# Local attention layers: steps of two head pairs, block transposes on VectorE, value products on 32x64 tiles

## The reference, cut to what matters

```python
def local_attention(q, k, v):                 # per head, nw = 8 windows of w = 32 queries
    bk2, bv2 = look(bk), look(bv)             # own window and the one before: 64 keys
    sim = einsum('bhwie,bhwje->bhwij', bq, bk2) * 8
    sim = where(mask, -max, sim)
    attn = softmax(sim, -1)
    return einsum('bhwij,bhwje->bhwie', attn, bv2)
def attn_layer(x, Wqkv, qs, ksc, Wo):
    q, k, v = split(x @ Wqkv)                 # 128 -> 3 x 1024
    q, k = l2norm(q) * qs, l2norm(k) * ksc    # then rotary tables with a scale
    ...
    return local_attention(q, k, v) @ Wo
def ffn_layer(x, g, bln, W1, b1, W2, b2):
    xn = layernorm(x) * g + bln
    a, gate = split(xn @ W1 + b1)             # 2 x 341
    return a * gelu(gate) @ W2 + b2
for i in range(6):
    x = attn_layer(shift_tokens(x)) + x
    x = ffn_layer(shift_tokens(x)) + x
```

## Time and profile before

| | us |
|---|---|
| median of 3 runs | 3802.07 (3801.65 to 3807.49) |
| the profiled execution, span | 3799.8 |
| first raw rows of the stage | near 1905 |
| one unit in the steady part | 38.18 |

### The profile page before, as it was taken

How to read it: one execution, slowest core, us unless ns; L and a number is a source line. 1 busy time by engine, 2 the same in 40 slices (tenths; PEclk the granted TensorE clock), 3 DMA queues, 4 the chain that set the end, 5 groups by cost and what they waited for, 6 DMA issues and landing times.

```text
span 3799.8 us, 102343 instructions
## 1 busy us (share of the span) xinstructions
PE 3156.4 (83%) x41325; PEld 2042.2 (54%) x41325; DVE 2683.2 (71%) x7106; ACT 2234.7 (59%) x5603; POOL 1457.8 (38%) x1443
## 2 busy tenths in 40 slices
PE   7878876727767879877679999999999999999997
PEld 5544544612323546545446666666666666666665
DVE  6466656537896554579787878777777777777773
ACT  4234442426554332268757777777777777777775
POOL 0110011336572000000066665656665666565651
PEclk9989987968897989989899999999999999999997
DMA  1000002710000000000001011101110201111110
GB/s 54 1 5 1 2 12 54 228 65 0 0 1 5 2 1 1 14 17 1 30 21 32 22 32 51 32 22 42 41 32 22 61 22 29 54 29 24 28 26 22
DMA packets 50453, 108.05 MB, mean 28 GB/s; under 512 B 7376, under 2 KB 17488, under 8 KB 48192
## 3 DMA queue, kind: packets, MB, share of 16 engines
q1 hardware_dynamic: 47456, 96.33, 9.3%
q0 software_dynamic: 2528, 5.18, 0.7%
HBM read 52.27 MB, written 5.18 MB: 15 GB/s over the span
## 4 chain that ended last, share of the span: by engine, by line
PE 45%; DVE 23%; ACT 13%; issue 6%; POOL 3%; DMA 1%; POOLq 0%; SPq 0%; DVEq 0%; ACTq 0%
PE psum L3240 5%; PE psum L3297 5%; PE psum L403 5%; PE psum L3280 4%; PE psum L1218 4%; PE psum L3190 4%; PE psum L408 3%; PE psum L2071 3%; DVE scratch L3452 2%; DVE xnT L3606 2%; PE psum L1272 2%; DVE xnT L3489 2%; ACT L3356 1%; PE psum L3265 1%; DVE scratch L3454 1%
## 5 line engine op out<-in xcount | busy, mean ns | idle before, releaser
L3646 POOL TENSOR_TENSOR scratch<-scratch 128x512 f32<-128x512 f32 x384 | 488.4, 1272 | 409.1 <-DVE scratch L3455 409.1
L408 PEld LDWEIGHTS psum<-table,scratch 128*128 128x128 f32 (+1 forms) x2284 | 283.1, 145 | 294.2 <-issue 234.1
L3297 PE MATMUL psum<-weights,scratch 128*128 128x512 f32 x768 | 413.6, 621 | 15.0 <-ACT y L3392 14.5
L408 PE MATMUL psum<-table,scratch 128*128 128x128 f32 (+1 forms) x2284 | 370.1, 283 | 44.5 <-DVE scratch L2772 11.8
L3659 POOL TENSOR_TENSOR scratch<-scratch,xnT 128x512 f32<-128x512 f32 x384 | 402.2, 1047 | 0.0
L3452 DVE TENSOR_TENSOR scratch<-psum,xnT 128x512 f32<-128x512 f32 x384 | 264.3, 688 | 146.0 <-PE psum L3297 139.4
L3426 ACT COPY scratch<-psum 128x512 f32<-128x512 f32 x384 | 225.8, 588 | 155.7 <-PE psum L408 149.8
L3392 ACT ACTIVATE y<-psum 128x512 f32<-128x512 f32 x384 | 230.9, 601 | 104.9 <-DVE scratch L3455 91.9
L3606 DVE TENSOR_REDUCE xnT<-y 128x8 f32<-128x512 f32 x384 | 253.9, 661 | 1.4
L1218 PE MATMUL psum<-scratch 32*128 32x256 f32 (+1 forms) x2560 | 180.2, 394 | 72.2 <-DVE weights L1479 22.2
L3581 DVE TENSOR_REDUCE scratch<-psum 128x4 f32<-128x256 f32 x384 | 161.1, 420 | 72.6 <-PE psum L3265 71.2
(11 more groups left out here) (550 smaller groups left out, 7632.6 us busy)
## 6 DMA issues: line engine op xcount, KB each, us to landing
scratch<-scratch SPq DMA_DIRECT2D x96, 256.0 KB
scratch<-experts_dram SPq DMA_DIRECT2D x47, 384.0 KB
scratch<-scratch SPq DMA_DIRECT2D x96, 128.0 KB
weights<-layer_dram SPq DMA_DIRECT2D x6, 1357.0 KB, 9.8
weights<-layer_dram SPq DMA_DIRECT2D x6, 1356.5 KB, 7.2
scratch<-scratch SPq DMA_DIRECT2D x96, 64.0 KB
weights<-gqa_dram SPq DMA_DIRECT2D x2, 1738.5 KB, 8.8
results_dram<-scratch SPq DMA_DIRECT2D x11, 256.0 KB
```

What stands on the lines that cost most here:

```text
L408: return self.nc.tensor.transpose(out, src, self.c("ident")[0:k, 0:k])
L3297: mm(raw_bank(a), window(m)[:, i * P:i * P + P], weight(m, "wqkv")[:, at:at + 512], start=True, stop=True).then_inc(S("rows_made").up(), 1)
L3646: gtt(out, out, sines, ALU.add).then_inc(S("rope_sum").up(), 1)
```

## The change

A step is now two pairs of heads ("double step"): the maxima, exponentials, sums, quotients and copies are of 512 columns where they were of 256, `STEPS` is 192, and all five programs are reordered by hand over `doubles`. V stays in the order of the tokens: own rows in `own`, the rows of the window before in `before`, which SP fills with two DMAs a unit. VectorE transposes the quotients in blocks of 32x32 in one instruction. The values are then products with 32 keys each, own and previous keys added up in PSUM; the four row strips write to four banks (4 to 7), in which raw rows (6), turned rows (5 and 4), V (5 and 7) and `third` (7) also have their place. The Newton step goes to GpSimd in four instructions. Both table loads fall into one double step.

```diff
-        wv = T(wqkv[:, 2 * LIN:].reshape(DIM, LHEADS // 2, 2, LDIM), (0, 2, 1, 3)).reshape(DIM, LIN)
...
-    STEPS, PARTS = PAIRS_L * UNITS, 8 * UNITS
+    STEPS, PARTS = PAIRS_L // 2 * UNITS, 8 * UNITS
...
+    RAW, ROOM, ROWS_T, SIDE = (0, 6), 1, (5, 4), 7
+    scores = M.psum[:, 2:4, 0:4 * 64]
+    SUMS = M.psum[:, 4:8, 0:4 * QB]
...
+    OFFSET = dict(project=(11, 12), added=12, center=13, moment=14, var=14, diagonal=16, ones=18, scaled=18,
+                  gates=22, third=22, third_gated=23, linear=23, gated=24, out=24, fed=26)
...
+    def pe_scores(D):
+        n, pair = D // 4, 2 * (D % 4)
+        pe.wait_ge(S("qk_out"), 8 * n + 4 * (pair // 4) + 3)
+        pe.wait_ge(S("exped"), D - 1)
+        for h in range(2):
+            mm(scores[:, h, :], ident, mask, start=True, stop=False, skip_group_check=True)
+        for pp in range(2):
+            for j in range(2):
+                for q in range(4):
+                    i, at = 4 * j + q, 64 * (2 * pp + j)
+                    for h in range(2):
+                        on = slice(64 * h, 64 * h + 64)
+                        last = mm(scores[QB * q:QB * q + QB, h, at:at + 64], QT[n % 2][on, pair + pp, i * QB:i * QB + QB],
+                                  KT[n % 2][on, pair + pp, i * QB:i * QB + 2 * QB], start=False, stop=True, skip_group_check=True)
+    def pe_values(D, s):
+        pe.wait_ge(S("turned"), D)
+        pe.wait_ge(S("qk_out"), min(s + 4, PARTS - 1))
+        pe.wait_ge(S("squared"), min(s + 15, PARTS - 1))
+        pe.wait_ge(S("v_out"), v_issued(s - 1))
+        pe.wait_ge(S("gathered"), D - 1)
+        for pp in range(2):
+            for j in range(2):
+                for kh in range(2):
+                    for h in range(2):
+                        at = (2 * (pair + pp) + h) * LDIM
+                        for q in range(4):
+                            on = slice(QB * q, QB * q + QB)
+                            last = mm(SUMS[64 * h:64 * h + 64, q, QB * (2 * pp + j):QB * (2 * pp + j + 1)],
+                                      (own if kh else before)[n % 2][on, j, at:at + LDIM], T[on, 4 * h + 2 * pp + j, kh, :],
+                                      start=(kh == 0), stop=(kh == 1), skip_group_check=True)
...
+        mm(M.bank(bank), window(n)[:, j * P:j * P + P], weight(n, "wqkv")[:, at:at + 512], start=True, stop=True)   # pe_v
...
+        for s in doubles:                       # TensorE
+            if 0 <= s // 2 < STEPS:
+                pe_scores(s // 2)
+            if 0 <= values_at(s) < STEPS:       # values_at(s) = s // 2 - 1
+                pe_values(values_at(s), s)
+            pe_fills(s, 0)
+            pe_raw(s + 16)
+            pe_fills(s, 1)
+            pe.wait_ge(S("gathered"), min(values_at(s), STEPS - 1))
+            pe_rows(s + 5)
+            pe_third(s)
+            vs = v_fills(s)
+            for v in vs[:-1]:
+                pe_v(*v)
+            pe_raw(s + 17)
+            for v in vs[-1:]:
+                pe_v(*v)
+            pe_rows(s + 6)
+            pe_fills(s, 2)
+            pe_fills(s + 1, 0)
...
+        for s in doubles:                       # ScalarE
+            D, t = s // 2, values_at(s)
+            if 0 <= D < STEPS:
+                act.wait_ge(S("bounded"), D)
+                act_exp(D, range(0, 5))
+            if 0 <= t < STEPS:
+                act.wait_ge(S("valued"), t)
+                copy(sums[t % SUMS_HELD].rearrange("p (x q i) -> p x q i", x=4, q=4),
+                     SUMS.rearrange("p q (x i) -> p x q i", x=4)).then_inc(S("gathered").up(), 1)
+            if 0 <= D < STEPS:
+                act_exp(D, range(5, 8)).then_inc(S("exped").up(), 1)
+            act_guess_of(s - 1)
+            act_guess_of(s)
+            act_fills(s)
+            act_rows(s + 5)
+            act_square(s + 16)
+            act_rows(s + 6)
+            act_square(s + 17)
...
+        for s in doubles:                       # VectorE
+            D = s // 2
+            if 0 <= D < STEPS:
+                dve.wait_ge(S("scored"), D)
+                red(by_head(small[D % 2][:, 0, :]), scores.rearrange("p h (x k) -> p h x k", x=4), AX, ALU.max, negate=True)
+            dve_fed(s)
+            dve_lens(s + 14)
+            dve_lens(s + 15)
+            dve_gated(s)
+            dve_var(s)
+            if 0 <= D < STEPS:
+                dve.wait_ge(S("exped"), D)
+                red(total, E[D % 2], AX, ALU.add).then_inc(dve.link(), 1)
+                nc.vector.reciprocal(total, total).then_inc(S("inverted").up(), 1)
+            dve_added(s)
+            dve_rope(s + 16)
+            dve_scaled(s)
+            dve_third(s)
+            dve_third(s + 1)
+            dve_rope(s + 17)
+            if 0 <= D < STEPS:
+                dve.wait_ge(S("divided_pool"), D)
+                dve.wait_ge(S("valued"), D - 1)
+                nc.vector.transpose(T.rearrange("p x k i -> p (x k i)"), E[D % 2].rearrange("p x k -> p (x k)"))
...
+    def pool_exact(s):
+        gtt(t, x, y, ALU.mult).then_inc(pool.link(), 1)
+        gtt(t, t, y, ALU.mult).then_inc(pool.link(), 1)
+        nc.gpsimd.tensor_scalar(t, t, -0.5, 1.5, ALU.mult, ALU.add).then_inc(pool.link(), 1)
+        gtt(y, y, t, ALU.mult).then_inc(S("inverse").up(), 1)
...
+            if s % 2 == 0 and 0 <= D < STEPS:
+                pool.wait_ge(S("inverted"), D)
+                gtt(E[D % 2], E[D % 2], over_keys(small[D % 2][:, 1, :]), ALU.mult).then_inc(S("divided_pool").up(), 1)
...
+            nc.sync.dma_start(before[n % 2][QB:P], own[n % 2][0:P - QB]).then_inc(moved.up(), 16)
+            nc.sync.dma_start(before[n % 2][0:QB, 1], own[n % 2][P - QB:P, 0]).then_inc(moved.up(), 16)
```

More of the change, by code:

```diff
@@ L3113, in part @@
+    by_head = lambda ap: ap.rearrange("p (h x) -> p h x", h=2)
+    over_keys = lambda ap: ap.unsqueeze(2).broadcast_to([P, 8, 64])
     def part(a):
         return a // 8, a % 8 // 4, a % 4 // 2, a % 2
[L3118 to L3127, removed]
@@ L3140, in room_for, with unit_root @@
+    def unit_root(n):
+        return order[("half" if n + 3 < UNITS else "unit", n + 3, 0)]
+    room, last_room = Bench(M, (ROOM,)), Bench(M, (RAW[0],))
     def room_for(key, n):
-        return last_room if n == UNITS - 1 and key[0] != "v" else room
+        return last_room if n == UNITS - 1 and key != "set" else room
     def room_of(key, n):
         return room_for(key, n).bank((key, n))
[L3146 to L3165, removed]
@@ L3427, in act_program @@
[L3427 to L3442 removed]
+                act.wait_ge(S("projected"), 2 * (t - SUMS_HELD) + 1)
@@ new lines, in act_set, with act_v @@
+    def act_set(s):
+        if set_at(s - 5) is not None:
+            e = set_at(s - 5)
+            k = len(tiles_of(e))
+            _, r = numbers_of(k)
+            act.wait_ge(S("y_scaled"), e)
+            for i in range(k):
+                last = nc.scalar.activation(done[e % 2][:, i, :], done[e % 2][:, i, :], ACT.Identity, bias=r[:, 1, i:i + 1],
+                                            scale=lengths[e % 2][:, 1, 66 + i:67 + i])
+            last.then_inc(S("yn_act").up(), 1)
+    def act_v(n, v, bank):
+        j, half = divmod(v, 2)
+        act.wait_ge(S("v_made"), 4 * n + v)
+        act.wait_ge(S("valued"), 4 * (n - 2) + 3)
+        copy(own[n % 2][:, j, 512 * half:512 * half + 512], M.bank(bank)).then_inc(S("v_out").up(), 1)
@@ L3470, in stage_local, with dve_lens @@
-    roots = [root_of(s)[:2] for s in steps if root_of(s)]
-    def dve_clamp(s):
-        m, half, first, last = root_of(s)
-        x = lengths[m % 2][:, 0, first:last]
-        if last > 66:
+    def dve_lens(a):
+        if not 0 <= a < PARTS:
+            return
+        m, q = divmod(a, 8)
+        dve.wait_ge(S("squared"), a)
+        dve.wait_ge(S("normed"), 8 * (m - 2) + 7)
+        red(lengths[m % 2][:, 0, 2 + 8 * q:10 + 8 * q], heads(sq[a % 2]), AX, ALU.add).then_inc(S("lens").up(), 1)
@@ L3614, in pool_rope, with dve_sets @@
+    def dve_sets(s):
+        for since, work in SET_WORK.items():
+            if set_at(s - since) is not None:
+                work(set_at(s - since))
+    CLEARS = 7
     def pool_rope(l):
```

627 lines of the change are left out of this document (303 added, 324 removed).

## The result

The changed kernel takes **3912.37 us** in the median of four runs (3889.86 to 3928.74), the kernel before 3801.86 on the same chip (3800.60 to 3807.49): ratio 1.029, 95% interval 1.025 to 1.0329. It is slower; forecast were 3610, faster with 0.86, and a range of 3550 to 3785. The changed kernel also scatters by 1%, the old one by 0.2% (on another chip by 0.5%). The profiled execution is the one of 3928.74 us, the slowest of the four.

What follows compares the result with a forecast made beforehand. TensorE's own work was taken as the bound: 31.7 work plus 2.4 idle gives 34.1 us a unit against 38.18; 4.08 x 47 = 192, so 3799.8 - 192 + 2.3 = 3610 us. Range 3550 to 3785.

Steps and rivals of the forecast that it cites:

- Values: ... 128 records are 16 rounds: 0.93 + 0.15 = 1.08: TensorE's values group per double step: eight tiles run together in 58 ns rounds, 1.08 us against 1.30 for two old groups.
- idle time of 2.4: TensorE's waits per unit: 0.5 copy of sums, 0.65 table loads, 0.6 semaphores before values, 0.6 before ones and gates.
- TensorE's work at full clock: TensorE's busy time per unit of the last stage: falls from 35.95 to 31.7 us.
- Scores: TensorE's scores per double step: one group of 64 records for two of 32, one drain less, 0.63 us.
- Masks: TensorE's masks per double step: two of 256 columns for four of 128, taken as 0.31 us.
- The loop: Rival: the chain through VectorE and ScalarE (7.2 us a double step against TensorE's 7.9) becomes the bound; 3709 us, chance 0.18.
- signs of being wrong: Values over 2 us, block transpose over 1.3, or TensorE waiting over 1 us in every double step.
- The block transpose: VectorE's transpose of 512 columns, four a unit: taken as 0.63 us each, adding 2.5 us a unit.
- VectorE is at 28.3 for 27.2: VectorE's busy time per unit: from 30.0 to 27.2 us, with the Newton step gone and four block transposes added.
- a narrow product has a price of its own: Rival: each of 128 value records costs 20 ns as now, 2.6 us a step; slower, 3897 us, chance 0.09.
- four tiles at a time: Rival: four rather than eight value tiles run together on TensorE, 2.0 us a step; 3784 us, chance 0.07.
- a dear block transpose: Rival: VectorE's block transpose costs as a reciprocal does, 3.5 us instead of 0.63; slower, 4033 us, chance 0.03.

Runs made afterwards that it cites:

- e1: The changed kernel with the value products of the previous 32 keys left out, 64 value records a double step instead of 128; measured 3602.86 us.
- e6: The changed kernel with quotients, their block transpose and both value buffers in bf16, one record a product instead of two; measured 3613.96 us.
- e8: The kernel before with every values product issued four times, 128 records a step on 64x64 tiles; 4495.72 us in a single run.
- e2: The changed kernel with the move of previous-window value rows cut to 64 of 1024 columns; measured 3849.49 us.
- e5: The kernel before with only the Newton step of the inverse lengths moved from VectorE to GpSimd, as four operations; measured 3779.00 us.

## Why the prediction was wrong

The step that failed is the term "Values: ... 128 records are 16 rounds: 0.93 + 0.15 = 1.08", and with it the idle time of 2.4, which knew no wait without a releaser, and a clock that stays at 1.00. Per unit, against the 34.1 of the forecast:

- *TensorE's work at full clock*: 34.05 for 31.7. Values are 1.42 for 1.08 a double step (+1.4 a unit). My reading of the earlier trace rows took the first slices for the whole group. Of the group at 2954.47 the first 32 records start within 0.24 us, as I had it; the next 96 take 1.03, 10.7 ns each, and 0.15 follows as drain. The kernel after, most of that group in three slices:

```profile
2954.47:2954.69 0.22, 0.22 (x28) 0.22 (x32) 1.00 0.00 0
2954.69:2955.10 0.41, 0.41 (x65) 0.41 (x52) 1.00 0.00 0
2955.10:2955.50 0.40, 0.40 (x66) 0.40 (x52) 1.00 0.00 0
```

  (A slice also counts records that began before it.) Scores are 0.79 for 0.63 (+0.6): the drain that I subtracted was for 32 records, and 64 don't keep the first ones' pace either. Masks came at 0.31 as stated, V at 0.86 for the 0.96 stated (-0.4). The old values group, read at 0.65 in the earlier trace rows, takes 0.60 in most steps, so 0.4 a unit less was there to save; +0.4 is spread over the rest.
- *Pauses for instructions*: 86.5 us in 24 units, 3.6 a unit (the issue rows of TensorE), forecast 0. This is the unforeseen mechanism, shown by e1, e6 and e8.
- *Clock*: 2.5 a unit, forecast 0 (sized by e1).
- *Other idle time*: 0.9 for 2.4. The loop through VectorE and ScalarE never bound the stage here; in e1 and e6, where TensorE is fast, the total of 2.64 and 3.19 is near the 2.4 that I had worked out.

Together 34.1 + 2.35 + 3.6 + 2.5 - 1.5 = 41.05, the measured unit, and (41.05 - 38.19) x 47 = 134 us against the 127.6 between the two spans (the medians are 110.5 apart). Without pauses and clock the sum would be 34.05 + 2.64 = 36.7 a unit, (38.19 - 36.7) x 47 = 70 us faster than before, about 3730: the mis-sized term alone would have stayed inside the range. The supply of instructions turned the sign. The signs of being wrong that the prediction named did not come: values are not over 2 us, the block transpose is not over 1.3, and TensorE waits over 1 us in fewer than half of the double steps, not in every one.

The other steps held. The block transpose is 698 ns long, 0.63 from start to start, for 0.63:

```profile
L3643 DVE STREAM_TRANSPOSE xn<-xn 128x512 f32<-128x512 f32 x96 | 67.0, 698 | 0.0
...
L3565 DVE TENSOR_SCALAR scratch<-scratch 128x34 f32<-128x34 f32 x12 | 10.2, 850 | 0.0
```

VectorE is at 28.3 for 27.2. The Newton step did go, but the price of standing beside GpSimd's operation passed on to the clamp of 34 columns (L3565), now 850 ns at that width: it starts 0.47 us behind GpSimd's rope addition of 1.27 and ends 0.04 behind its end. The clamps took 0.4 us a unit and take 1.3, most of the 1.1. ScalarE 25.9 for 26.0, GpSimd 24.3 for 24.8.

Of the rivals, "a narrow product has a price of its own" named the outcome (3897) but not the cause: a record costs 11 ns, not 20, and the 17 ns from which it decides were not reached. The loop, four tiles at a time, and a dear block transpose did not occur. What I could have seen: 24576 more instructions for TensorE's values (12288 matmuls and their loads), and a queue of instructions on the page that I never divided by anything. The earlier trace rows hold 64 records in 1.04 us at the densest, followed by wide work; the change puts 192 into 2.2.

The page Runtime: NRT & Kernel Launch of the Trainium skill ("Instruction fetch mechanics") says that an engine fetches the next block of 256 instructions, 16 KiB, while it executes the current one, and that crossing a block is mostly hidden. The trace agrees on the block (256 instructions, 16 KB). It is hidden before, and not in the kernel after, where 81 pauses stand behind block starts.

## What to carry to other kernels

Before a product is cut into narrower ones, count the instructions, loads and matmuls, of the densest 3.5 us: here kernels with up to 284 ran with one pause at most and those with 346 or more did not, with blocks of 256. A number for a long group must not be taken from its first records, and idle time put down to "issue" in the middle of a group was here a matter of supply, not a dependency. Where narrow tiles are wanted, operands that need one record and not two made them pay here (e6), at the cost of precision.

## What the runs showed of the hardware

- Value records of different 32x64 tiles start 8 ns apart for the first 32 (0.24 us) and 10.7 ns apart from there on (1.03 us for 96); 64 in bf16 take 0.61 us from start to start, 128 in fp32 1.42.
- After a pause of 1.96 us without a record the granted clock was at 0.50 in the following stretch of 2.7 us; of 81 pauses 55 had such a stretch behind them. Over the stage it fell from 1.00 to 0.92, which cost 2.5 us a unit.
- The eleven pauses of 3.3 to 5.3 us all met hundreds of KB of other transfers, and their blocks started 0.9 to 2.8 us after TensorE had stopped; with the small move (e2) the longest pause was 2.7 us.
- The clamp of 34 columns takes 850 ns (L3565) where it now meets GpSimd's rope addition; in e5 the same clamp (L3481) has a mean of 205 ns over both of its widths, 34 and 32 columns.
- The block transpose of 128x512 fp32 on VectorE: 698 ns.
